# Attention on one core: TensorE's order taken from a search that charges for changes of tiling, and block outputs in two PSUM banks by turns

## What is computed

```python
def _L0_attn_ref(x, Wq, bq, Wk, bk, Wv, bv, Wo, bo):
...
    q = x @ Wq.T + bq
    k = x @ Wk.T + bk
    v = x @ Wv.T + bv
    split = lambda z: z.reshape(b, t, h, hd).transpose(0, 2, 1, 3)
    q, k, v = (split(q), split(k), split(v))
    q = apply_rope(q)
    k = apply_rope(k)
    scale = math.sqrt(hd)
    att = jnp.einsum('bhqd,bhkd->bhqk', q, k) / scale
    mask = jnp.tril(jnp.ones((t, t), dtype=bool))
    att = jnp.where(mask[None, None, :, :], att, -jnp.inf)
    att = jax.nn.softmax(att, axis=-1)
    y = jnp.einsum('bhqk,bhkd->bhqd', att, v)
    y = y.transpose(0, 2, 1, 3).reshape(b, t, d)
    y = y @ Wo.T + bo
    return y
...
    x = x + 0.5 * _L0_ffn_ref(_layernorm(x, axis=-1), ...)
    x = x + _L0_attn_ref(_layernorm(x, axis=-1), ...)
    x = x + 0.5 * _L0_ffn_ref(_layernorm(x, axis=-1), ...)
```

## Time and profile before

| | us |
|---|---|
| median of 3 runs (1580.44 to 1582.68) | 1581.53 |
| the profiled execution, its own time | 1581.88 |
| its span | 1579.0 |
| first exponential of attention starts | 587.3 |
| last exponential of attention starts | 1100.5 |

### The profile page before, as it was taken

How to read it: one execution, slowest core, us unless ns; L and a number is a source line. 1 busy time by engine, 2 the same in 40 slices (tenths; PEclk the granted TensorE clock), 3 DMA queues, 4 the chain that set the end, 5 groups by cost and what they waited for, 6 DMA issues and landing times. The chain is left out here.

```text
span 1579.0 us, 26583 instructions
## 1 busy us (share of the span) xinstructions
PE 1495.6 (95%) x9977; PEld 1034.3 (66%) x9977; DVE 889.0 (56%) x1962; ACT 982.2 (62%) x1332; POOL 552.4 (35%) x478
## 2 busy tenths in 40 slices
PE   4899999999998979999999999999799999999997
PEld 3788888888887853333333333333578888988896
DVE  6888676666655961113044332122788857766673
ACT  7422254455434879999999999998532235444542
POOL 3000245666544971112121122120300045566644
PEclk9999999999998989999999999999999999999999
DMA  8231256666645789405246353120413136666653
GB/s 276 74 107 54 69 157 147 153 152 158 145 79 151 249 275 171 77 7 82 38 86 106 98 83 59 26 68 27 159 48 110 51 116 156 149 152 155 153 121 40
DMA packets 121376, 181.04 MB, mean 115 GB/s; under 512 B 19040, under 2 KB 83040, under 8 KB 118496
## 3 DMA queue, kind: packets, MB, share of 16 engines
q1 hardware_dynamic: 92784, 130.56, 31.7%
q0 software_dynamic: 28464, 48.78, 15.2%
HBM read 123.73 MB, written 55.57 MB: 114 GB/s over the span
## 5 line engine op out<-in xcount | busy, mean ns | idle before, releaser
L2001 ACT ACTIVATE 8258_pr<-8258_pS 128x1024 f32<-128x1024 f32 x448 | 421.8, 1082 | 12.7 <-PE 8258_pS L1922 11.4
L1952 PE MATMUL 8258_pO<-8258_pr,6357_vres 128*32 128x512 f32 x1792 | 239.3, 606 | 4.6 <-DVE 8258_tO L2026 3.3
L1922 PEld LDWEIGHTS 8258_pS<-sq_rows,sk_rows 50*128 50x128 f32 x896 | 74.8, 185 | 202.9 <-ACT 8258_pr L2001 159.2
L1922 PE MATMUL 8258_pS<-sq_rows,sk_rows 50*128 50x512 f32 x896 | 186.2, 466 | 10.0 <-PEq L1554 5.5
L2026 DVE STREAM_TRANSPOSE 8258_tO<-8258_pO 128x512 f32<-128x512 f32 (+1 forms) x33 | 23.0, 699 | 258.8 <-PE 8258_pO L1952 256.0
L190 PE MATMUL 115_pGU<-columns_XT,weights_wts 128*128 128x512 f32 x384 | 152.7, 398 | 1.8 <-DVE columns_XT L959 1.6
L190 PE MATMUL 15225_pGU<-columns_XT,weights_wts 128*128 128x512 f32 x384 | 152.7, 398 | 1.8 <-DVE columns_XT L959 1.6
L2015 POOL TENSOR_SCALAR_AFFINE_SELECT 8258_pr<-8258_pr 128x512 f32<-128x512 f32 x32 | 21.2, 662 | 367.7 <-ACT 8258_pr L2001 367.6
L191 PE MATMUL 115_pGU<-columns_XT,weights_wts 128*128 128x512 f32 x384 | 149.7, 390 | 0.0
L191 PE MATMUL 15225_pGU<-columns_XT,weights_wts 128*128 128x512 f32 x384 | 149.7, 390 | 0.0
L192 PE MATMUL 15225_pGU<-columns_XT,weights_wts 128*128 128x512 f32 x384 | 149.6, 390 | 0.0
(11 more groups left out here) (393 smaller groups left out, 3390.8 us busy)
## 6 DMA issues: line engine op xcount, KB each, us to landing
115_raw_g<-WgT SPq DMA_DIRECT2D x16, 512.0 KB
115_raw_u<-WuT SPq DMA_DIRECT2D x16, 512.0 KB
115_raw_d<-WdT SPq DMA_DIRECT2D x16, 512.0 KB
q_rows<-rows_halves SPq DMA_DIRECT2D x8, 1024.0 KB, 5.0
k_rows<-rows_halves SPq DMA_DIRECT2D x8, 1024.0 KB, 5.1
15225_raw_g<-WgT SPq DMA_DIRECT2D x16, 512.0 KB
15225_raw_u<-WuT SPq DMA_DIRECT2D x16, 512.0 KB
15225_raw_d<-WdT SPq DMA_DIRECT2D x16, 512.0 KB
```

Source lines behind the costliest of these rows:

```text
L1922: m = t_.matmul(to[:, e, :], key, query, start=True, stop=True)
L1952: m = t_.matmul(pO[e * 32:(e + 1) * 32, off:off + wd], vres[:, (g // GB) * TPB + kt, at:at + 32], from_(e), start=n == first[j], stop=n == ...
L2001: s_exp.done(a.activation(to, pS[:, u % RING, :, :], ACT.Exp, scale=HD ** -0.5))
```

## The change

- The single pass is replaced by a search (`Planner`). It keeps a state of TensorE, ScalarE and GpSimd with times in microseconds, extends it by scores, items or a piece, and holds the 100 best states in each window. Going from one kind of matmul to another adds `DRAIN` 0.114, and scores behind another kind `KEYS` 0.12 more. The best state's steps become `slot`, `split_at`, `piece_at`.
- `pO` has two banks; block j uses bank j % 2. A piece goes into the bank of the block that ended last (`piece_behind`), and `pT` is gone. So the first item of block j waits for the turning of block j - 2 and for the additions of the pieces in its bank; a piece waits for the turning of the block whose bank it takes, and still for the addition of the piece before it.
- Two pieces more are inside the loop; late are (7,1,0) and (7,1,1).
- The fill of one half of `sk` with ones at the start of the stage is VectorE's first instruction and no longer GpSimd's, with a semaphore of its own.

```diff
--- before.py
+++ after.py
...
+class Planner:
+
+    EXP, EXP_ENDS, SCORED, VALUED, FREED = 0.905, 1.03, 0.21, 0.1, 0.08
+    DRAIN, KEYS, SCORES, ROWS, VALUES, PIECE = 0.114, 0.12, 0.213, 0.026, 0.427, 0.78
+    COPY, ADD, MASK, MASK_IN, MASK_OUT = 3.0, 1.5, 0.65, 0.1, 0.8
+    WAITING, LATE, WIDTH, RUN = 0.6, 2.0, 100, 3
...
+    def scores(self, o):
+        u, at = o.S, o.pe
+        if u >= self.ring:
+            if u - self.ring >= len(o.exps):
+                return None
+            at = max(at, o.exps[u - self.ring] + self.FREED)
+        n = o.then("S")
+        if o.mode != "S":
+            n.pe = at + (self.DRAIN if o.mode else 0.0) + self.KEYS + self.SCORES
+        else:
+            n.pe = at + (self.KEYS if at > o.pe else 0.0) + self.SCORES
+        n.scored.append(n.pe)
+        n.S, n.mode = u + 1, "S"
+        self.exponentials(n)
+        return n
+
+    def values(self, o):
+        i = o.V
+        if i >= self.NI or self.source[i] >= len(o.exps):
+            return None
+        at = max(o.pe, o.exps[self.source[i]] + self.FREED)
+        if self.mask_of[i] is not None:
+            if self.mask_of[i] >= len(o.masked):
+                return None
+            at = max(at, o.masked[self.mask_of[i]] + self.MASK_OUT)
+        if i in self.first:
+            at = max(at, o.bank[self.first[i] % 2])
+        n = o.then("V", self.window(o))
+        start = at if o.mode == "V" else max(at, o.pe + self.DRAIN)
+        n.pe = start + 2 * (self.VALUES * self.share[i] + self.ROWS)
+        n.valued.append(n.pe)
+        n.V, n.mode = i + 1, "V"
+        if i in self.final:
+            n.occupy(self.final[i] % 2, n.pe + self.COPY)
+            n.ended[self.final[i]] = self.window(o)
+        self.exponentials(n)
+        return n
+
+    def piece(self, o):
+        k, w = o.P, self.window(o)
+        if k >= len(self.pieces) or o.mode == "P" or self.piece_block[k] not in o.ended:
+            return None
+        begin = None
+        if self.pieces[k][2] == 0:
+            begin = max(o.free + 1, o.ended[self.piece_block[k]] + 1)
+        if w < (begin + 5 if begin is not None else o.free + 4):
+            return None
+        j = max(o.ended)
+        n = o.then("P", w, begin, j)
+        n.pe, n.mode, n.P, n.free = max(o.pe + self.DRAIN, o.bank[j % 2]) + self.PIECE, "P", k + 1, w
+        n.occupy(j % 2, n.pe + self.ADD)
+        return n
+
...
+    def plan(self):
+        o = Order()
+        for _ in range(self.ring):
+            o = self.scores(o)
+        level = [o]
+        for w in range(self.NU - self.ring):
+            reached = {}
+            for o in level:
+                o = self.scores(o)
+                for _ in range(self.RUN + 1):
+                    if o is None:
+                        break
+                    for c in (o, self.piece(o)):
+                        if c is not None:
+                            late = c.act + self.EXP * (w + 4 - len(c.exps)) + self.WAITING * self.waiting(c)
+                            reached.setdefault((c.V, c.P, c.mode), []).append((late, c))
+                    o = self.values(o)
+            ranked = []
+            for some in reached.values():
+                some.sort(key=lambda a_: (a_[0], a_[1].pe))
+                kept = []
+                for late, c in some:
+                    if len(kept) < 3 and (not kept or c.pe < kept[-1].pe - 1e-9):
+                        kept.append(c)
+                        owed, n = 0.0, c.V
+                        while n < self.NI and self.source[n] < len(c.exps) - 1:
+                            owed += 2 * self.VALUES * self.share[n]
+                            n += 1
+                        ranked.append((late + 0.35 * max(0.0, c.pe + owed - late - 1.0) + 0.02 * owed, c))
...
+            ranked.sort(key=lambda a_: a_[0])
+            level = [c for _, c in ranked[:self.WIDTH]]
+        ends = []
+        for o in level:
+            while o is not None and o.V < self.NI:
+                o = self.values(o)
+            if o is not None:
+                ends.append(o)
+        o = min(ends, key=lambda a_: a_.pe + self.LATE * (len(self.pieces) - a_.P))
+        steps = []
+        while o.before is not None:
+            steps.append(o.step)
+            o = o.before
+        steps.reverse()
+        slot = [st[1] for st in steps if st[0] == "V"]
+        put = [st for st in steps if st[0] == "P"]
+        piece_at = {st[1]: p for st, p in zip(put, self.pieces)}
+        split_at = {st[2]: p[:2] for st, p in zip(put, self.pieces) if st[2] is not None}
+        return slot, split_at, piece_at, {p: st[3] for st, p in zip(put, self.pieces)}
...
-            pO = t.ps("pO", [P, 512])
-            pT = t.ps("pT", [P, 512])
+            pO = t.ps("pO", [P, 2, 512])
...
-            EXP, PAIR, VALUE, PIECE = 90, 34, 25, 90
-            slot, piece_at, split_at = [], {}, {}
-            spent, w, free = 0, 0, 0
-            while len(slot) < len(items):
-                spent = max(spent, EXP * (w - 1)) + (PAIR if w + RING < NU else 0)
-                more = True
-                while more and len(slot) < len(items):
-                    n = len(slot)
-                    j, what, s = items[n]
-                    wide = 4 if what == "whole" else 4 - s
-                    until = unit_of[2 * (s + NR)] - 2 if what == "whole" and s + NR < len(whole) else NU
-                    more = known[n] <= w and (spent + wide * VALUE // 2 <= EXP * (w + 1) or w >= until)
-                    if n == first[j] and j:
-                        more = more and w >= slot[-1] + 2
-                    if more:
...
-                w += 1
-            NW = w
+            source = [unit_of[2 * s + 1] if what == "whole" else source_of(j, s) for j, what, s in items]
+            share = [1.0 if what == "whole" else (4 - s) / 4 for j, what, s in items]
+            mask_of = [mask_no.get(i_) for i_ in items]
+            frees = [([item_no[whole[a_ // 2 - NR][0], "whole", a_ // 2 - NR]] if a_ // 2 >= NR else []) if kind == "pair" else
+                     ([max(item_no[a_ - 2, "cut", c] for c in ((1, 3), (1, 3), (2,))[b_])] if a_ >= 2 else [])
+                     for kind, a_, b_ in units]
+            slot, split_at, piece_at, piece_behind = Planner(RING, source, share, mask_of, [m[0] for m in masks], frees,
+                                               {n: j for j, n in first.items()}, {n: j for j, n in final.items()},
+                                               pieces, [last_of(m, c) for m, c, r in pieces]).plan()
+            NW = slot[-1] + 1
...
@@ -1833,6 +1963,7 @@
             self.s_out = s_out = [sig(f"attn_out{k}", 16) for k in range(4)]
             self.s_table, self.s_ahead = sig("attn_table", 16), sig("attn_ahead", 16)
             s_ln, self.s_norm = sig("attn_dve_ln"), sig("attn_dve_norm")
+            s_ones = sig("attn_dve_ones")
...
-                sp.wait_ge(*self.s_clear.at(4))
+                sp.wait_ge(*s_ones.at(1))
                 for hh in range(GH):
                     self.load_head(sp, 1, hh, slice(0, S), self.s_ld[1][hh // 2])
...
                     if n == first[j]:
                         assert off == 0
-                        s_copy.wait(t_, j)
+                        s_copy.wait(t_, j - 1)
+                        s_free.wait(t_, max([place[p] + 1 for p, i in piece_behind.items() if i % 2 == j % 2 and i < j], default=0))
                     for e in range(GH):
                         at = ((g % GB) * GH + e) * VW
-                        m = t_.matmul(pO[e * 32:(e + 1) * 32, off:off + wd], vres[:, (g // GB) * TPB + kt, at:at + 32],
+                        m = t_.matmul(pO[e * 32:(e + 1) * 32, j % 2, off:off + wd], vres[:, (g // GB) * TPB + kt, at:at + 32],
                                       from_(e), start=n == first[j], stop=n == final[j])
                     s_O.done(m)
 
...
                         s_free.wait(t_, n_)
-                        to = pT[:, :]
+                        t_.wait_ge(*s_copy.at(piece_behind[m_, c, r] + 1))
+                        to = pO[:, piece_behind[m_, c, r] % 2, :]
...
 
             @blk.gpsimd
             def _(g):
-                self.s_clear.done(g.memset(sk[:, 1, :, :].bitcast(f32), 1.0))
                 for u, j, what, s in masks:
                     g.wait_ge(*s_exp.at(u + 1))
...
-                    s_copy.done(v.transpose(tO[:, part], pO[:, part]))
...
-                    from_ = at_end(m, c, r) if (m, c, r) in late else pT[:, :]
+                    from_ = at_end(m, c, r) if (m, c, r) in late else pO[:, piece_behind[m, c, r] % 2, :]
                     s_free.done(v.tensor_tensor(two, from_.rearrange("p (t d) -> p t d", d=D), two, ALU.add))
...
+                s_ones.done(v.memset(sk[:, 1, :, :].bitcast(f32), 1.0))
                 for n in range(NW):
```

56 lines of the change are left out of this document (38 added, 18 removed).

## The result

The changed kernel takes 1567.5 us (median of 4 runs, 1566.48 to 1568.24) beside 1580.99 (4 runs, 1579.28 to 1582.68): a ratio of 0.9908, interval 0.9892 to 0.9924. It is faster by 13.5 us; the forecast was 1562.5, 19.0 less, with a range of 1559.5 to 1571. Direction and range held, the gain came out 5.5 us smaller. The profiled execution took 1568.18 by its own clock, its span was 1566.1.

What follows compares the result with a forecast made beforehand. Attention was taken as bound by a chain of 544 exponentials on ScalarE, paced with TensorE. Gains of 16.7 (18.2 - 1.5, chain), 0.5 (start) and 1.8 (end) sum to 19.0: 1581.5 - 19.0 = 1562.5 us, range 1559.5 to 1571.

Steps and rivals of the forecast that it cites:

- The floor, 0.906 a step: Attention's exponentials on ScalarE: an undisturbed step takes 0.906 us, so 18.2 us are lost after the start, 3.0 in it.
- half of it: Rival: the planner's fixed costs differ from real ones, half of the 18.2 us loss stays, about 1570 us; chance 0.16.
- The residue of 1.5: Loss left in the chain of exponentials after the change, 1.5 us, put in the last forty windows; bounds 0 and 8.
- Slack by merging: TensorE in attention: fewer, merged groups of scores and values cut its work, raising slack against ScalarE from 2.6 to 12.1 us.
- Waits for an exponential longer in sum than before: Sign: TensorE, now having slack, would wait longer in sum for exponentials than in the kernel before.
- No stretch of 13 starts over 12.5 us: Sign: after the start, no stretch of 13 exponential starts on ScalarE would be longer than 12.5 us.
- The two banks: Attention's values: the first value's wait for VectorE's turning, 3.1 us in 15 waits, goes; pieces' new waits cost nothing.
- gatekeeper rival: Rival: each of 30 pieces waits for VectorE's turning and addition; at 2 us each, 17 us slower, 1598; chance 0.03.
- The start, 0.5: First 22 exponentials of attention: 0.5 us gained of 3.0 lost; bounds 2 lost and 1.5 gained.
- Fill, loads and stores at nothing: Moving the fill of ones to VectorE, and shifting windows of statistics, normalising and stores, gains or costs nothing.
- The end, 1.8: Behind attention's last exponential: 0.7 from an earlier turning, 0.7 from a piece wait, 0.4 from additions; bounds 1.0 and 2.4.
- It does not do what it says: Rival: ScalarE's steps are longer for its own reason, only 1.8 us at the end gained, 1579.7 us; chance 0.04.

Runs made afterwards that it cites:

- run 3: The changed kernel with the planner's charge for a change of tiling (DRAIN and KEYS) set to 0: 1605.31 us, ratio 1.0159 to the kernel before.
- Run 2: The changed kernel's new order with the old memory, all blocks in one bank and pieces in pT: 1578.07 us, ratio 0.9979 to the kernel before.
- run 1: The changed kernel with the old single-pass order put back, two banks kept: 1577.2 us, ratio 0.9973 to the kernel before.
- run 7: The changed kernel with the fill of ones back on GpSimd, in front of the masks: 1571.43 us.
- Run 10: The changed kernel with quarter 1's bias addition in window 84 and unread matmuls filling TensorE at attention's end: 1566.35 us, ratio 0.9904 to the kernel before.
- runs 5 and 9: 5: changed kernel, value matmuls except a block's first streaming three quarters of their columns, 1574.94 us. 9: changed kernel, 45 more exponentials behind the last addition, 1612.14 us.

## Why the prediction came out as it did

**The floor, 0.906 a step: wrong, and this is the step that failed.** It was read off starts over stretches of 14 and 12 steps. They looked undisturbed, and were; but I did not ask whether a start that is recorded 0.904 behind the last one means an exponential finished in 0.904. The lengths in the earlier trace rows, 1017 at least and 1402 at most, said that it need not. The second stretch was misread besides: from 1089.64 to 1100.48 it is twelve steps of 0.904, not 0.908, so that both stretches gave the same number and the bound of 0.908 had no row. With 0.917 the kernel before had lost 490.3 - 521 x 0.917 = 12.5 us behind the start, not 18.2, and 22.98 - 22 x 0.917 = 2.8 in it. The sum would have been 12.5 - 1.5 + 0.5 + 1.8 = 13.3, and the time 1568.2.

The range of 1559.5 to 1571 held, but nothing in it was drawn for a floor of 0.917: the floor's own bound was 0.9036, which makes the gain larger, and the upper part was there for a larger residue and for "half of it", neither of which came. As far as the floor goes, that the range held is luck.

**The residue of 1.5: right.** 0.96 and 0.95 were measured, in four steps; the largest (0.40) was not TensorE's order alone but GpSimd beside VectorE. **Slack by merging: there, but its sum does not decide.** TensorE has time now, in the changed kernel for instance:

```profile
707.53 0.91 PE L2053 MATMUL 8258_pS<-sq_rows,sk_rows 50*128 50x512 f32 x4
708.36 1.07 PE L2084 MATMUL 8258_pO<-8258_pr,6357_vres 128*32 128x512 f32 x8
709.36 0.91 PE L2053 MATMUL 8258_pS<-sq_rows,sk_rows 50*128 50x512 f32 x4
```

The cycle takes 1.83, ScalarE's two steps, and the pair of scores 0.83 of it, where it takes 0.67 when nothing holds it up. The matmul's record covers this wait, so that TensorE is recorded busy 483.67 of 485 us all the same. But run 3 has nearly as few changes and is slower than the kernel before. What the prediction said of the shape, no lone units in a row, goes with the loss in all three orders. The prices of 0.19 and 0.13 a merge were tested by no run. "Waits for an exponential longer in sum than before" was a wrong sign: they fell from 156.7 to 132.6. By my own numbers TensorE stands still for 513.2 - 489.4 = 24 before and 496 - 479.9 = 16 after; the stage shrinks by more than the work. Fewer waits in a shorter stage was to be expected.

**"No stretch of 13 starts over 12.5 us": narrowly wrong**, 12.76 at the longest (from 1068.83) against 13.64 before. 13 steps at 0.917 are 11.9, and a recorded start falls back up to 0.24 by itself.

**The two banks: right that the wait goes and that pieces do not wait**; nothing in the waits of a piece names VectorE. Undersold: the prediction put the banks' worth at the 3.1 us of waits and the empty windows behind them. Run 2 shows that without them the new order loses 9.8. Of the gatekeeper rival the runs show nothing.

**The start, 0.5: about right in size**, 0.56 and 0.86 by ends; what makes it is not shown, and it is not the order, since run 1 with the old one loses the same 2.3. **Fill, loads and stores at nothing: right for the fill (run 7)**; for loads and stores no wait of the chain names one, and no run varied them.

**The end, 1.8: too large; 1.1 to 1.2.** From the last exponential's start to the end of the last addition it is 9.6 us, not 8.9, where before has 10.7. It is inside the bounds given (1.0 to 2.4), but one of its terms was empty. On VectorE in order of time:

```profile
1092.06 0.78 DVE L2158 STREAM_TRANSPOSE 8258_tO<-8258_pO 128x256 f32<-128x256 f32 x2 [10.11 <-PE 8258_pO L2084]
...
1096.72 0.69 DVE L2201 TENSOR_TENSOR rows_acc<-8258_pS,rows_acc 128x512 f32<-128x512 f32 x1
1098.66 0.69 DVE L2201 TENSOR_TENSOR rows_acc<-8258_pS,rows_acc 128x512 f32<-128x512 f32 x1 [1.26 <-PE 8258_pS L348]
```

The turning starts 2.3 us behind the last exponential's start instead of 3.1, the 0.8 as foreseen (0.7). From there to the end it is 7.29 (1092.06 to 1099.35) where the earlier trace rows has 7.64 (1103.59 to 1111.23): 0.35 gained, not 1.1. Before, additions ran while TensorE did its last piece, so that taking two away uncovers its end, and now VectorE waits 1.26 for that piece, which runs at the low clock (0.42 a matmul instead of 0.28): of the 4.9 us between the last value and this piece TensorE stood still for 3.9. Run 10 gets 0.67 back by filling them.

**The rivals.** "Half of it" gave 1570, and 1567.5 lies nearer to that than to 1562.5. Its mechanism is absent all the same: debts reach ScalarE at four places, not at many, and runs 5 and 9 speak against the rest. Its condition, that merges are worth only the page's drain, was tested by no run. A time near a rival's is no proof of the rival. "It does not do what it says" had the right suspicion, that a step is longer for ScalarE's own reasons, by about a third of the size it needed (0.011 us a step, where 18.2 over 521 steps are 0.035).
